# Moving one of conv 2's four subtractions a step from VectorE to GpSimd in a two-layer depthwise convolution kernel

## What is computed

```
x = x + conv3x3(group_norm(x), L0_conv_k)            # pad 1
w_sym = (w + rot90(w,1) + rot90(w,2) + rot90(w,3)) * 0.25
x = x + conv7x7(group_norm(x), w_sym)                # pad 3
```

## Time and profile before

| | |
|---|---|
| median of three runs | 3190.64 us |
| the profiled execution's own time | 3185.82 us |
| its span | 3184.0 us |
| TensorE busy | 2851.3 us, 90% |
| VectorE busy | 2818.7 us, 89% |
| ScalarE busy | 2161.2 us, 68% |
| GpSimd busy | 2188.2 us, 69% |
| DMA engines | 224 GB/s in the mean |
| granted TensorE clock, mean | 0.974 of 2.4 GHz |

### The profile page before, as it was taken

The page is one execution under the profiler, slowest core; times in us unless marked ns, Lnnn a source line. Parts: engine busy times, 40 slices in busy tenths (PEclk is TensorE's granted clock), DMA queues, the critical chain, the costliest instruction groups (busy, mean ns, idle before and its releaser), DMA issues.

```text
span 3184.0 us, 76492 instructions
## 1 busy us (share of the span) xinstructions
PE 2851.3 (90%) x28676; PEld 1805.6 (57%) x28676; DVE 2818.7 (89%) x5372; ACT 2161.2 (68%) x3969; POOL 2188.2 (69%) x2321
## 2 busy tenths in 40 slices
PE   0388999999999999999999999999999999999996
PEld 0155655565555655666665666655666665556663
DVE  3377999989999999999999999998999999999985
ACT  1175777777777776777777777776777776777771
POOL 3165767776777776777767677766777777777773
PEclk9898999999999999999999999999999999999997
DMA  3599888888888888888988888898888898888876
GB/s 89 139 237 232 234 233 232 233 228 224 229 234 232 240 236 216 238 231 232 243 223 237 227 239 236 231 241 223 226 230 244 231 237 227 232 237 227 241 174 174
DMA packets 966521, 712.45 MB, mean 224 GB/s; under 512 B 102918, under 2 KB 904710, under 8 KB 966086
## 3 DMA queue, kind: packets, MB, share of 16 engines
q1 hardware_dynamic: 511494, 383.52, 46.2%
q10 hardware_dynamic: 405504, 201.38, 22.3%
q0 software_dynamic: 49152, 122.65, 15.9%
HBM read 259.73 MB, written 220.81 MB: 151 GB/s over the span
## 4 chain that ended last, share of the span: by engine, by line
DVE 30%; POOL 22%; DMA 16%; issue 13%; PE 7%; ACT 6%; ACTq 3%; SPq 3%; DVEq 0%; POOLq 0%
POOL H L638 17%; DMA BT<-H 15%; DVE H L466 6%; DVE X L483 6%; DVE BT L506 5%; DVE BN L475 5%; PE PS L735 4%; PE PS L768 3%; POOL H L660 3%; ACTq L568 3%; ACT Z L557 2%; ACT H L554 2%; POOL BT L652 2%; SPq L268 2%; DVE TMP L429 1%
## 5 line engine op out<-in xcount | busy, mean ns | idle before, releaser
L735 PE MATMUL PS<-H,BAND 128*128 128x512 f16 x6912 | 1576.4, 388 | 79.4 <-DMA BAND<-rows 69.3
L735 PEld LDWEIGHTS PS<-H,BAND 128*128 128x128 f16 x6912 | 1019.6, 150 | 611.7 <-issue 100.1
L660 POOL TENSOR_TENSOR H<-Z,H 128x512 f16<-128x512 f32 x768 | 839.7, 1094 | 731.5 <-ACT Z L557 730.8
L768 PE MATMUL PS<-BT,BAND 118*32 118x512 f16 x21504 | 1258.2, 389 | 65.5 <-issue 37.2
L768 PEld LDWEIGHTS PS<-BT,BAND 118*32 118x32 f16 x21504 | 756.1, 132 | 521.8 <-issue 165.5
L554 ACT ACTIVATE H<-X,RB 128x512 f16<-128x512 f32 x768 | 619.4, 806 | 467.8 <-DVE H L466 439.2
L638 POOL TENSOR_SCALAR H<-X,RB 128x512 f16<-128x512 f32 x768 | 877.8, 1152 | 82.1 <-DVE RB L437 68.0
L506 DVE COPY BT<-BT 39x4256 f16<-39x4256 f16 x384 | 567.5, 1478 | 146.6 <-DMA BT<-H 136.8
L557 ACT ACTIVATE Z<-X,RB 128x512 f32<-128x512 f32 x768 | 615.5, 801 | 0.0
L537 ACT ACTIVATE Z<-X,RB 128x512 f32<-128x512 f32 x768 | 561.3, 802 | 30.4 <-issue 23.9
L580 ACT ACTIVATE DUMP<-X 128x512 bf16<-128x512 f32 x768 | 472.7, 617 | 149.2 <-DVE X L483 143.7
(11 more groups left out here) (48 smaller groups left out, 510.1 us busy)
## 6 DMA issues: line engine op xcount, KB each, us to landing
X<-in_x SPq DMA_DIRECT2D x768, 256.0 KB, 5.6
out_y<-X ACTq DMA_DIRECT2D x768, 256.0 KB, 6.6
BT<-H POOLq DMA_DIRECT2D x384, 162.1 KB, 5.2
BT<-H POOLq DMA_DIRECT2D x384, 149.6 KB, 5.2
BT<-H SPq DMA_DIRECT2D x576, 99.8 KB
BT<-H SPq DMA_DIRECT2D x384, 62.3 KB
BT<-H SPq DMA_DIRECT2D x192, 83.1 KB
rows<-v_all SPq DMA_DIRECT2D x8, 1638.0 KB, 11.2
```

The costliest lines, as they stand in the source:

```text
L660: g.tensor_tensor(part(H1, n, 1, img, O1, P1), Z[:, img, :].rearrange("p (c w) -> p c w", c=CC), part(H1, n, 0, img, O1, P1), ALU.subtract ...
L735: last = mm(PA[:, ch, :], band[:, j, ws, :], data[:, :, O1 - 1 + j:O1 - 1 + j + W], start=k == 0, stop=k == 3 * K1 - 1)
L768: last = mm(banks2(n)[b * BL:(b + 1) * BL, ch, :], band[:, j, :], rows, start=j == 0, stop=j == K2 - 1, tile_position=(0, b * BL))
```

## The change

GpSimd takes the low part of the last image (`last_low2`), behind the four issues of `gather_high` and ahead of `low_parts1`. VectorE keeps the first three. A new semaphore `last_low` counts the moved subtraction, and those who waited for all four counts of `lo_done[1]` now wait for three counts and for `last_low`: SyncE ahead of the gathers of the low rows, and ScalarE ahead of the last image of `normalise1`, and of `normalise2` in the last steps.

```diff
@@ SyncE, slot
-                    wait_apart(sp, lo_done[1], NI * at(n) + NI)
+                    sp.wait_ge(lo_done[1], (NI - 1) * (n + 1))
+                    sp.wait_ge(last_low, n + 1)
                     gather_low(n)
@@ VectorE, slot
                 n = t - 4
                 if real(n):
-                    for img in range(NI):
+                    for img in range(NI - 1):
                         m = NI * at(n) + img
                         dve.wait_ge(normed[1], m + 1)
                         dve.wait_ge(hi_done[1], m + 1)
@@ ScalarE
+            def wait_low2(n, img):
+
+                if n >= 0 and img == NI - 1:
+                    act.wait_ge(last_low, n + 1)
+                elif n >= 0:
+                    act.wait_ge(lo_done[1], (NI - 1) * n + img + 1)
+
...
-                        act.wait_ge(lo_done[1], m - NI + img + 1)
+                        wait_low2(n - 1, img)
...
                 if real(n - 5):
-                    act.wait_ge(lo_done[1], m - 5 * NI + img + 1)
+                    wait_low2(n - 5, img)
@@ GpSimd
+            def last_low2(n):
+
+                pool.wait_ge(normed[1], NI * n + NI)
+                pool.wait_ge(hi_done[1], NI * n + NI)
+                g.tensor_tensor(part(H2, n, 1, NI - 1, O2, P2), Z[:, NI - 1, :].rearrange("p (c w) -> p c w", c=CC),
+                                part(H2, n, 0, NI - 1, O2, P2), ALU.subtract).then_inc(last_low, 1)
+
...
                 if real(t - 4):
                     high_parts2(t - 4, at)
                     gather_high(t - 4)
+                    last_low2(t - 4)
                 if real(t + 1):
                     low_parts1(t + 1, at)
```

More of the change, by code:

```diff
@@ L155, in conv_program @@
         lo_done = [sem("lo_done1"), sem("lo_done2")]
+        last_low = sem("last_low")
         conv1_done, conv2_done = sem("conv1_done"), sem("conv2_done")
```

## The result

The change made the kernel slower. The changed kernel ran in 3283.41 us (median of four, 3282.03 to 3291.64) against 3195.11 us for the kernel before, run on the same chip: a ratio of 1.0284, with a 95% interval of 1.025 to 1.0318. The forecast was 3170 us, the range 3138 to 3207. One execution in all that follows was slow, 4488 us at a granted clock of 0.626, in the version of "Who goes first in step C"; it is left out of that version's median and ratio.

The account below looks back on a forecast made before the run. The bounding loop was taken as VectorE's copies of A, its work up to L437, GpSimd's high parts and the DMAs. (0.12 + 0.12) x 64 = 15 us and 6 us made 21 us less: 3170 us, range 3138 to 3207.

Parts of the forecast that it names:

- The loop and what hides the relief: Copies of step A, VectorE's work up to L437, GpSimd's high parts, DMAs; of 115 us relief, waits leave 21 us.
- one free unit in six in A: In step A one unit in six has no wait for the high rows and keeps 0.60 us: 6 us.
- L429's wait in C: Due at 1037.61 in step C, L429 waits for GpSimd's last L660 until 1038.25, leaving 0.12 us a unit.
- Step B, the first subtraction: In step B VectorE's first subtraction waits for GpSimd's, losing 0.48 us of 0.60: 0.12 us a unit left.
- Step C: VectorE's third subtraction goes before GpSimd's, which ends near 1033.4; after L429's wait 0.12 us a unit is left.
- a sign of being wrong: The third subtraction of step C over 1.5 us long would show the forecast wrong.
- The rival that named this: GpSimd gets the memory first in step C; VectorE's third subtraction starts 0.93 us late: 3204 us, chance 15%.
- Step A: VectorE's three subtractions end before GpSimd's starts, so they don't meet; copies wait 0.60 us longer for the high rows.
- TensorE's wait for it: TensorE's wait at L707 for VectorE's L496 in step A should shrink from 45.5 us.
- VectorE's wait for the high rows: VectorE's wait ahead of its copies should grow from 99.7 us in 2400 by some 25.
- the two faster rivals: High rows land sooner in step A, 3147 us, 18%; subtractions don't hold each other up, 3139 us, 10%.
- the low rows: Slower rival: TensorE waits in step B for low rows coming 1.06 us later from step A: 3225 us, 9%.

Follow-up runs that it names:

- Who goes first in step C: Subtraction moved in step C alone, GpSimd also waiting for VectorE's second subtraction there, against the kernel before: 3191.43 us, ratio 1.0.

## Why the prediction was wrong

- **The loop and what hides the relief: right in kind, and it hides more than predicted.** I counted 0.12 us in B, 0.12 in C and one free unit in six in A, 21 us. With the work left out it was 8 us. L429's wait in C showed there (0.67 us where I said 0.5 to 0.7). In the changed kernel it didn't, 0.16 us in the unit above, since VectorE came late. And the 0.16 us that I took for before were one unit: in 19 of 54 units it was already held then. In B I had counted all of the 0.60 us against the first subtraction's wait, and missed that the copies too, when they come earlier, run into GpSimd's last L660.
- **Step B, the first subtraction: right in kind and size** (1.25 us; I had 1.16). The term was still wrong: to the 0.57 us lost there come 0.6 us of the copies, so the step is 0.54 us longer and not 0.12 shorter. The sum for that step never asked what GpSimd's later L660 would meet.
- **Step C is the step that failed:** 1.20 us longer, where I had 0.12 shorter. "I take it that VectorE goes first." The two starts were 0.02 us apart, and I let a start-up time of 0.1 us, read from one high part behind a copy, decide. GpSimd went first in 50 of 54 steps, and moving it back by 0.17 us turned it round. Its moved subtraction took 1.18 us there and not some 1.6, and VectorE's third 1.58, which I had named as a sign of being wrong.
- **The rival that named this was priced too low.** I had 0.93 us of delay for one GpSimd instruction, 0.21 us a unit after the other terms, 3204 us. The trace has 2.56 us: the second subtraction is held too, and the L660 behind it takes the port a second time, since GpSimd's next instruction was ready without a gap. `RB` of that step is written 1.94 us later after the first subtraction (10.41 us from 8.47 in the median). GpSimd's own slack of 1 us is in that, and 1.20 us a unit remain.
- **Step A: the subtractions don't meet in most units, as said.** In the changed kernel they met in 1 of 53, with A moved alone in 11. What I left out was GpSimd's next high parts: 1 us later, they meet L496, which takes 0.72 us for 0.17. TensorE's wait for it (L707, L724 now) did not shrink from 45.5 us but doubled to 91.2. VectorE's wait for the high rows fell to 57.9 us instead of growing by 25, which fits a VectorE that is late everywhere else.

```profile
DVE BT L508 <- DMA BT<-H: 57.9, 41, 3.1
```

- **The sizes of the chances.** The range ended at 3207 because the unknown price of a meeting was bounded by one instruction's length. (The sums are off by a hundredth: 0.27 and the two faster rivals are 0.55, and the low rows with a third of the win in C are 0.14.) The nearest rows were about meetings of a long operation with a four-element one, or with a copy, never of two long ones with another waiting behind.

## What to carry to other kernels

Before work goes from VectorE to GpSimd, list for each of its new places what VectorE runs beside it. Operations with two operands in SBUF, even of four elements, and copies like L506 were stretched here beside a GpSimd instruction that reads, and a queue on GpSimd that is ready to go on can hold one VectorE instruction for three of its own. List too what GpSimd's next instructions meet, once they are later or earlier than before; several versions here failed by that. Recorded starts did not settle who is held: GpSimd won with a start up to 0.6 us behind VectorE's and lost with one 0.16 us behind. Treat the order of two instructions that overlap as unknown, price the bad one in full, with the next instruction of each engine, and put a wait in that fixes it; it cost nothing here and took back 2.8%. And leave the work out once before moving it: that run shows what the move can bring where the rest stays as it is.

## What the hardware did that I had not expected

- A GpSimd subtraction of 512 columns that started 0.59 us into a VectorE one, which follow one another every 0.60 us, kept it from ending for 1.65 us more (2.33 us for 0.68), and was itself not slowed (1.18 us; 1.17 in B, where it meets one that starts later).
- One that started 0.52 us into VectorE's last subtraction of a step held it through three GpSimd instructions in a row (4.34 us for 0.68).
- Started 0.16 us into the third, it was the one that waited (1.54 us) and the time was that of before.
- Half the columns cost about as much as all (ratios 1.018, with VectorE's four, and 1.0192, with three), 16 columns nothing that could be measured.
- Four-element operations with two inputs in SBUF, 0.16 us alone, took 0.72 us beside GpSimd's high parts and 1.14 us beside its subtraction.
- The same stretch of GpSimd filled with writes alone (1.16 us) did not touch VectorE's subtractions.
